# The correction of the second layer on 32x128 tiles of the array, in place of 32x32 tiles

## The reference

```python
pos = grid_q[:, :, None, :] - grid_kv[:, None, :, :]
bias = jnp.sign(pos) * jnp.log1p(jnp.abs(pos))
bias = jax.nn.relu(bias @ cpb_w1 + cpb_b1)
bias = jax.nn.relu(bias @ cpb_w2 + cpb_b2)
bias = (bias @ cpb_w3 + cpb_b3).reshape(b, GROUPS, H * W, Hd * Wd)
sim = jnp.einsum('bhid,bhjd->bhij', qh, kh) + bias
attn = jax.nn.softmax(sim, axis=-1)
```

## Time and profile before

| | before |
|---|---|
| median of 3 runs | 914.47 us (913.43 to 914.48) |
| the profiled execution: its own time | 915.55 us |
| its span in the profile | 913.5 us |
| mean granted clock of TensorE | 0.97 of full speed |
| busy: PE, PEld | 848.0 us (93%), 290.2 us (32%) |
| busy: DVE, ACT, POOL | 711.9 us (78%), 657.2 us (72%), 71.2 us (8%) |
| L797, float32 part of the second layer, PE | 352.3 us busy |
| L792, correction, PE | 127.4 us busy |
| L811, third layer, PE | 277.0 us busy |

### The profile page before, as it was taken

One profiled execution on the slowest core, in us unless ns is written; L12 is line 12 of the kernel. 1 busy time (PEld: TensorE's weight loads), 2 busy tenths in 40 slices (PEclk: granted clock), 3 DMA queues, 4 the chain that ended last, 5 costly groups with the idle time before them and its releaser, 6 DMA issues.

```text
span 913.5 us, 33809 instructions
## 1 busy us (share of the span) xinstructions
PE 848.0 (93%) x15524; PEld 290.2 (32%) x15524; DVE 711.9 (78%) x493; ACT 657.2 (72%) x773; POOL 71.2 (8%) x40
## 2 busy tenths in 40 slices
PE   2299999899999999899999999989999999999986
PEld 1133233333333333323333333323333333333322
DVE  4699698898877688899885878889887768888811
ACT  2368678867776687887776877886777768777761
POOL 2120003210000004040000001240000000000000
PEclk8589999999999999999999999999999999999998
DMA  3301001020020101002020101002020010200000
GB/s 148 89 20 40 13 2 52 7 53 5 9 58 14 50 3 50 8 3 56 3 64 14 49 4 33 20 8 54 5 57 20 8 46 2 74 3 3 3 15 35
DMA packets 23804, 27.44 MB, mean 30 GB/s; under 512 B 15600, under 2 KB 17520, under 8 KB 23664
## 3 DMA queue, kind: packets, MB, share of 16 engines
q1 hardware_dynamic: 23664, 25.29, 10.4%
HBM read 23.05 MB, written 2.10 MB: 28 GB/s over the span
## 4 chain that ended last, share of the span: by engine, by line
issue 56%; PE 30%; POOL 6%; DVE 3%; DMA 2%; ACT 2%; SPq 0%; ACTq 0%; POOLq 0%; DVEq 0%
PE pair L797 10%; PE scores L811 9%; PE pair L792 4%; POOL conv_prod L315 3%; POOL big L422 3%; PE pair L934 2%; DVE h L589 1%; PE pair L943 1%; PE scores L821 1%; PE pair L918 1%; DMA att_den<-reciprocals_dram 1%; PE pair L900 1%; ACT h L442 1%; PE scores L906 1%; PE pair L925 0%
## 5 line engine op out<-in xcount | busy, mean ns | idle before, releaser
L442 ACT ACTIVATE h<-pair 128x1024 f32<-128x1024 f32 x512 | 496.4, 1021 | 189.9 <-PE pair L797 184.5
L589 DVE TENSOR_TENSOR h<-hx,hy 128x2048 f32<-128x2048 f32 x256 | 581.3, 2301 | 37.7 <-PE pair L797 37.4
L797 PE MATMUL pair<-h,wts 32*32 32x512 f32 x8192 | 352.3, 601 | 6.9 <-DVE h L589 6.8
L811 PE MATMUL scores<-h,wts 128*32 128x512 f32 x2048 | 277.0, 613 | 0.1
L792 PE MATMUL pair<-fy,u_rows 32*32 32x512 bf16 x4096 | 127.4, 387 | 29.6 <-DMA fy<-fy_dram 16.8
L797 PEld LDWEIGHTS pair<-h,wts 32*32 32x32 f32 x8192 | 134.0, 103 | 26.7 <-DVE h L589 10.2
L811 PEld LDWEIGHTS scores<-h,wts 128*32 128x32 f32 x2048 | 40.6, 108 | 218.5 <-issue 216.0
L792 PEld LDWEIGHTS pair<-fy,u_rows 32*32 32x32 bf16 x4096 | 40.0, 88 | 200.4 <-issue 170.0
L315 POOL TENSOR_TENSOR conv_prod<-qpad,wts 128x288 f32<-128x288 f32 x16 | 31.3, 1985 | 425.6 <-ACT qpad L469 425.6
L422 POOL TENSOR_TENSOR big<-big,hat_x 128x512 f32<-128x512 f32 x16 | 37.2, 2350 | 119.1 <-DVE big L687 119.1
L716 DVE TENSOR_REDUCE neg_max<-pair 128x8 f32<-128x512 f32 x32 | 22.1, 690 | 29.7 <-PE pair L900 29.3
(11 more groups left out here) (89 smaller groups left out, 381.1 us busy)
## 6 DMA issues: line engine op xcount, KB each, us to landing
hx<-features_dram SPq DMA_DIRECT2D x64, 128.0 KB, 2.8
hy<-features_dram SPq DMA_DIRECT2D x64, 128.0 KB, 3.2
att_den<-reciprocals_dram SPq DMA_DIRECT2D x8, 256.0 KB
wts<-weights_dram SPq DMA_DIRECT2D x2, 960.0 KB, 7.7
x<-x_dram SPq DMA_DIRECT2D x2, 512.0 KB, 5.4
fy<-fy_dram SPq DMA_DIRECT2D x64, 6.0 KB
fy<-fy_dram SPq DMA_DIRECT2D x64, 4.0 KB
fy<-fy_dram SPq DMA_DIRECT2D x64, 2.0 KB
```

The lines of the kernel that those rows point to most:

```text
L442: emptied("z", 2 * g + j, act.activation(h2[g % H2_BUFS][:, 2 * j:2 * (j + 1)].rearrange("p r n -> p (r n)"), pair_of("z", 2 * g + j)[:], ...
L589: dve.tensor_tensor(h1[g % H1_BUFS][:].rearrange("p c (y x) -> p c y x", x=W), hx[unit % 2][:, :, t].unsqueeze(2).broadcast_to([128, CT, H ...
L797: ins = pe.matmul(z[r][32 * c:32 * (c + 1)], w(l, "w2")[key[r], key[r]], h1[g % H1_BUFS][key[r], c], start=False, stop=True)
L811: ins = pe.matmul(scores[phase % 2][32 * r:32 * (r + 1)], w(l, "w3")[:, 32 * t:32 * (t + 1)], h2[g % H2_BUFS][:, r], start=t == 0, stop=t ...
```

## The change

The matmuls of the correction have 32 rows and 32 columns of weights each: for each r, four of them read the same `y` and neighbouring columns of `u_rows`, and write neighbouring 32 partitions of the same bank. The change makes one matmul of them for each r, with 32 rows and 128 columns of weights.

```diff
                     y = fy[unit % 2][key[r], t, H // 2 * h:H // 2 * (h + 1)]
-                    for c in range(CT):
-                        pe.matmul(z[r][32 * c:32 * (c + 1)], u_rows[l][key[r], 32 * c:32 * (c + 1)],
-                                  y.unsqueeze(2).broadcast_to([32, H // 2, W]), start=True, stop=False)
+                    pe.matmul(z[r], u_rows[l][key[r]], y.unsqueeze(2).broadcast_to([32, H // 2, W]), start=True, stop=False)
                 pe.wait_ge(h1_ready, g + 1)
```

## The result

| | before | after |
|---|---|---|
| median, 8 runs each | 914.44 us (909.67 to 916.0) | 923.08 us (918.33 to 926.1) |
| ratio after to before | | 1.0098, 95% interval 1.0069 to 1.0128 |
| profiled execution: its time, its span | 915.55 us, 913.5 us | 926.1 us, 924.2 us |
| mean granted clock of TensorE | 0.97 | 0.967 |

The change makes the kernel 0.98% slower, 8.6 us on the medians. The forecast was 931.5 us with a range of 919 to 942, so the direction and the range hold, and the 17 us that were forecast are twice what came.

What follows compares the result with a forecast made beforehand. PE, going from group to group without a wait, was taken as the bound; plain steps +14.2, transposition steps +7.0, other-stage steps -4.1 and 34 others 0 gave +17.1 on 914.47, stated as 931.5 us, range 919 to 942.

Steps and rivals of the forecast that it cites:

- What bounds the kernel: PE goes from group to group without a wait; plain steps of 2.49 us follow its distances, the ring barely not holding.
- (1) Fewer matmuls and loads: In the correction, twelve of sixteen matmuls and loads go, saving only some 0.04 us between first and last start.
- (2) The change of form: Before L797, PE changes from 32x128 to 32x32 tiles once more a step and drains, taken at 0.09 us.
- (3) The load: L797's 128-column weight load can't run ahead of the form's change; taken at 0.045 us more, bounds 0 and 0.105.
- x: Time from the start of the correction's last waiting half, or of the group, to L797: 0.23 + 0.09 + 0.045 = 0.365 us.
- the rival of the quick load: The wider weight load before L797 costs nothing, so x = 0.32: +7.2 us, 921.7 us; chance 0.12.
- (4) A clean L797 and the ring's wait: L797 takes 1.08, losing 0.18 no more, but x follows the relu's wait: plain steps +0.145, transposition +0.225, other stages -0.045 us.
- The 34 other steps: Steps where ACT or DVE holds PE by more than the change, or where the terms cancel: 0.
- the rival without a drain: L797 starts after 0.275 and presses in for 1.27 as before; all 220 steps 0.045 longer: +9.9, 924.4 us; chance 0.07.
- That nothing changes: ACT's or DVE's chain holds PE anyway, so the time stays at 914.5 us; chance 0.05.
- that wide tiles don't overlap: In the correction, wide loads run one behind the other: 22.8 us more, 954.4 us; chance 0.06 together with a dear load.
- that the kernel gets faster: The form's change costs nothing but L797 runs in 1.08: 911.8 us at x = 0.275, 901.9 at 0.23; chance 0.08.

Runs made afterwards that it cites:

- experiment 5: Kernel before the change, with ACT's second-layer relu shortened to the first bank of each pair from step 3 on: 898.55 us, ratio 0.9834.
- Experiment 3: Kernel before the change, with the correction on eight 32x64 tiles a step in place of sixteen 32x32: 928.4 us, ratio 1.0157.
- Experiments 1 and 2: Kernel before the change, with only half of the correction on 32x128 tiles, the first half, then the second: 958.0 and 965.1 us, beside 914.3.
- Experiment 4: Kernel before the change, all 32x32 tiles, with PE made to wait for the correction's last matmul before L797: 971.0 us.
- experiments 5 and 6: The same shortened second-layer relu put into the kernel before and into the changed kernel: 898.55 us and 882.76 us, ratios to the kernel before 0.9834 and 0.9664.
- the halves in turn: Kernel before the change, reordered so each half's correction is followed by its own product before the other half: 1080.4 us, ratio 1.182.

## Why the forecast came out as it did

**What bounds the kernel** held. The plain steps kept to PE's distances, and experiment 5 left them at 2.49 when ACT's relus got shorter. That the steps add up to 10.3 of the 10.7 us shows nothing by itself, since they fill nearly the whole span.

**(1) Fewer matmuls and loads** don't pay for the change of form: there are 3072 fewer of both, and the kernel is 0.98% slower. What they are worth alone was not measured. Experiment 3 adds that eight matmuls are slower than four and than sixteen.

**(2) The change of form** costs what was taken. L795 follows a group that didn't wait after 0.32, which is the 0.23 of before and 0.09, if the load adds nothing, as its record says. Experiments 1 and 2 show it in both directions between 32x32 and 32x128.

**(3) The load** is the term that was mis-sized. It was taken at 0.045 from L900's float32 loads; its record is 91 ns against 88, and x is 0.32, not 0.365. In the forecast's own formula that is 220 x 0.32 - 63.2 = +7.2 us in place of +17.1. This was the rival of the quick load, to which 0.12 was given. The rule of the Trainium skill (TensorE: Matmul & The Clock Gate, Weight-path perf modes — Fast Weight Load (FWL) and DoubleRow), that the quick load is on for 128 columns that aren't FP32, agrees with 91 ns for 128 columns and 102 ns for 64. The Trainium skill's rule by the number of columns (the same page, LDWEIGHTS (loading the stationary operand)) doesn't fit these records: by it 128 columns take 80 ns more than 32, and they took 3 more.

**(4) A clean L797 and the ring's wait** came as forecast: 1.07 everywhere; plain steps 2.59 with x = 0.32 (1.19 + 0.32 + 1.08), 3.50 with the transposition (2.10 + 0.32 + 1.08), 0.08 less with another stage. Experiment 4 shows the first part, experiments 5 and 6 the second, by its sign.

**The 34 other steps** were put at 0 and gave 3.4 us in the profiled execution. Up to 2.7 us of that is at the two places with the longer stretch at the lower clock, which the forecast named and left out of the sum. The 220 steps of the formula gave 9.6 + 5.4 - 8.2 = 6.8 us against 7.2. In the spans that makes 10.3 with the rest, but the medians lie 8.6 apart, and the profiled execution had the lowest clock of its eight. How much the 34 steps cost in a usual execution is left open, so the formula is confirmed by the steps and not by the total.

**The other rivals.** By its time alone the rival without a drain (924.4) would fit 923.1 as well as the quick load (921.7). The steps decide: that rival had L795 0.275 behind L791 and 1.27 to L809, and they show 0.32 and 1.07. That nothing changes, that wide tiles don't overlap, and that the kernel gets faster did not occur. The last has its mechanism in the trace all the same: 0.08 us is saved in each of 91 steps.

## What to carry to other kernels

Count changes of the tiles' form on TensorE before matmuls: a group of another form waits until the last one has streamed, and what matters is whether that drain lies behind a wait that ends last. Where it does, it adds in full; where it doesn't, an emptied array can even pay, since a group that presses in behind occupied tiles may lose more. And test a wait by shortening what it waits for in both versions: here the sign of the difference turned, which no timing of the change alone could have shown.

## What the runs showed of the hardware that was not expected

- A weight load of 32x128 bf16 has a record of 91 ns, one of 32x64 102 ns and one of 32x32 88 ns.
- A float32 group of 16 tiles takes 1.07 to 1.08 us to the next group on an empty array, and 1.27 behind matmuls on the same tiles. Behind a half that had waited it takes 1.40. An exchange of its loops left the 1.27 as it was, and with the order turned round the sum stayed at 1.50.
- Matmuls for free tiles pass those for occupied ones. With the halves in turn all sixteen of the correction started before the first of the product (224.11 and 224.18 us for the last and the first), though in the program eight of them stand behind half of the product. Even so the product took 2.05 us and not 1.27.
- The 0.2 us that the float32 product loses behind the correction are lost by half of its tiles: eight start together, and the other eight 0.19 to 0.30 us behind the first.
- At the same wait of PE (2.36 us before, 2.85 after) the granted clock was at its lower level for 3.4 us in the profile before, and for 6.8 us in the one after. Among the eight executions of the changed kernel the time falls as the mean clock rises: 926.1 us at 0.967, 918.33 at 0.979.
